# Last stage of a two-block image kernel: one narrow projection for two pairs of images, and stacked rows filled by transfers

## What is computed

```python
r = jnp.einsum('bhwc,cd->bhwd', x, Wr) + br                  # 64 channels to 16
r = jax.nn.relu((r - mean) * jax.lax.rsqrt(var + BN_EPS) * gamma + beta)
w = jnp.einsum('bhwd,dk->bhwk', r, Ws) + bs                  # 16 to 9 taps x 16 groups
xi = jnp.einsum('bhwc,cf->bhwf', x, Wi) + bi                 # 64 to 64
patches = ...                                                # the 9 shifts of padded xi
out = jnp.sum(w * patches, axis=-1)                          # per group of 4 channels
```

## Time and profile before

| what | value |
|---|---|
| median of 3 runs | 675.14 us (674.09 to 675.57) |
| profiled execution, its own time | 673.33 us |
| its span, first to last instruction | 671.5 us |
| mean granted clock of TensorE | 0.985 |
| last stage: first tap of pair 0 to the end | 453.9 to 671.5 us |
| one pair in it, from pair 2 on | 12.74 us |

### The profile page before, as it was taken

How to read it: one execution, slowest core, us unless ns; L and a number is a source line. 1 busy time by engine, 2 the same in 40 slices (tenths; PEclk the granted TensorE clock), 3 DMA queues, 4 the chain that set the end, 5 groups by cost and what they waited for, 6 DMA issues and landing times. The chain is left out here.

```text
span 671.5 us, 15413 instructions
## 1 busy us (share of the span) xinstructions
PE 628.5 (94%) x5984; PEld 250.0 (37%) x5984; DVE 522.5 (78%) x816; ACT 326.7 (49%) x451; POOL 181.0 (27%) x193
## 2 busy tenths in 40 slices
PE   6868999889999999999999989798999999999995
PEld 7523333323333333333333323233444444444442
DVE  5699875997766666766688676969898898888885
ACT  3754632311422242133315545743687787788761
POOL 2100330007300810280047000531344234235231
PEclk9979899999999999999999979999999999999998
DMA  8930030042433253125422416000122222132132
GB/s 323 220 66 1 1 84 1 1 95 71 98 93 73 72 139 101 50 71 141 95 67 55 116 31 149 1 9 9 25 57 48 48 64 48 41 70 49 40 72 63
DMA packets 67461, 47.95 MB, mean 71 GB/s; under 512 B 53602, under 2 KB 54596, under 8 KB 67396
## 3 DMA queue, kind: packets, MB, share of 16 engines
q1 hardware_dynamic: 67108, 46.82, 28.3%
q10 hardware_dynamic: 288, 0.21, 0.1%
HBM read 35.15 MB, written 9.76 MB: 67 GB/s over the span
## 5 line engine op out<-in xcount | busy, mean ns | idle before, releaser
L759 PE MATMUL conv<-xpad,comb 64*64 64x512 f32 x2016 | 228.1, 597 | 4.3 <-DVE x L1386 4.2
L1646 DVE TENSOR_TENSOR x<-conv,x 128x512 f32<-128x512 f32 x288 | 177.9, 683 | 24.0 <-PE conv L814 22.7
L759 PEld LDWEIGHTS conv<-xpad,comb 64*64 64x64 f32 x2016 | 75.4, 134 | 136.6 <-issue 121.7
L814 PE MATMUL conv<-rstack,wse 98*128 98x512 f32 x288 | 95.9, 434 | 2.9 <-DVE xin L1432 0.9
L830 PE MATMUL att<-x,cmp 64*32 64x512 f32 x1280 | 79.7, 596 | 0.0
L814 PEld LDWEIGHTS conv<-rstack,wse 98*128 98x128 f32 x288 | 48.1, 188 | 72.3 <-DVE x L1646 65.7
L1318 DVE SCALAR_TENSOR_TENSOR xpad<-att,x 128x1024 f32<-128x1024 f32 x46 | 54.1, 1219 | 25.7 <-PE att L609 25.3
L960 ACT ACTIVATE x<-conv,bias 128x512 f32<-128x512 f32 x40 | 25.2, 682 | 90.5 <-PE conv L759 90.5
L728 PE MATMUL conv<-row_sums,comb 64*64 64x512 f32 x480 | 58.5, 617 | 9.0 <-DVE xin L1432 7.7
L1798 POOL TENSOR_TENSOR x<-x,xin 128x1024 f32<-128x1024 f32 x15 | 35.9, 2393 | 111.5 <-ACT x L1112 111.5
L951 ACT ACTIVATE comb<-experts,small 128x768 f32<-128x768 f32 (+1 forms) x33 | 27.4, 859 | 78.1 <-PE conv L728 31.9
(11 more groups left out here) (212 smaller groups left out, 749.8 us busy)
## 6 DMA issues: line engine op xcount, KB each, us to landing
experts<-forms SPq DMA_DIRECT2D x72, 192.0 KB, 4.0
experts<-forms SPq DMA_DIRECT2D x72, 144.0 KB, 2.8
x<-in_x SPq DMA_DIRECT2D x32, 256.0 KB, 5.6
out<-comb SPq DMA_DIRECT2D x30, 256.0 KB, 3.2
rstack<-rstack SPq DMA_DIRECT2D x16, 128.0 KB, 2.3
experts<-in_We SPq DMA_DIRECT2D x1, 1152.0 KB
forms<-experts SPq DMA_DIRECT2D x2, 576.0 KB, 5.7
out<-comb SPq DMA_DIRECT2D x4, 128.0 KB, 2.2
```

The costliest lines, as they stand in the source:

```text
L759: last = nc.tensor.matmul(conv[own[to], h, HW * rows:HW * rows + HW], comb[own[rows], q % 2, n, tap(t)], xpad[own[rows], 2 * (q % 2) + n, ...
L814: nc.tensor.matmul(conv[:, unit, cols], wse[:, ORDER[i], :], rstk[s][0:RR, cols], start=True, stop=True).then_inc(exp_full, 1)
L1646: v.tensor_tensor(img(prod[i])[:, rows, :], img(conv[:, unit, :])[:, rows, :], xip[s][:, kh + 16 * h:kh + 16 * h + 16, kw:kw + W], ALU.mul ...
```

## The change

The narrow projection is made for two pairs at once. `wr` has the block once, 32 columns wide, and four matmuls write the two halves of pairs k+1 and k+2 to four blocks of 32 partitions of `att[:, 1, 0:512]`. It is made in odd pairs only, behind the two sums and ahead of tap 2; the place behind tap 3 is gone. ScalarE normalises pair k+2 instead of k+1, takes relu and the rounded copy of both pairs as 128x512 (into `r_lo4` and `r_hi4`), and issues two of the transfers. GpSimd subtracts once for two pairs (`split_two`), ahead of the residual of pair k-1. The stacks are filled by transfers of 32 rows x 512 columns (64 KB): six for each pair, four of slot 0's and six of slot 1's on SyncE (`fill`), which waits for the expansions of pair k-2. `misc_*` counts five uses per two pairs. Some buffers move (`prod`, `xn`).

```diff
-        prod = [flat[:, n * S:(n + 1) * S] for n in (0, 1, 2, 3, 4, 5, 13, 14, 15)]
-        xn = [flat[:, (6 + n) * S:(7 + n) * S] for n in range(2)]
-        r64 = flat[0:TWO, 8 * S:9 * S]
+        prod = [flat[:, n * S:(n + 1) * S] for n in (0, 1, 2, 3, 4, 7, 13, 14, 15)]
+        xn = [flat[:, n * S:(n + 1) * S] for n in (6, 5)]
+        r_lo4 = flat[:, 8 * S:8 * S + HW]
+        r_hi4 = flat[:, 8 * S + HW:9 * S]
...
+        def misc_before(k):
+
+            return 5 * (k // 2) + (4 if k % 2 else 2)
...
-            copy_high(0, 0)
-            copy_high(1, 1)
+            def fill(k, s, made):
+
+                eng.wait_ge(rhi_ready, made)
+                if not (isinstance(k, int) and k < 2):
+                    eng.wait_ge(exp_full, 2 * TAPS * (k - 1))
+                for first, part in ((0, r_hi4), (ONE, r_lo4)) if s == 0 else ((0, r_hi4), (2 * ONE, r_hi4), (ONE, r_lo4)):
+                    if first == ONE:
+                        eng.wait_ge(rlo_ready, made)
+                    for h, cols in halves():
+                        rows = slice(2 * ONE * s + ONE * h, 2 * ONE * s + ONE * h + ONE)
+                        eng.dma_start(rstk[s][first:first + ONE, cols].bitcast(F32), part[rows, :]).then_inc(rstk_filled[s], 16)
+
+            for n in range(2):
+                fill(n, n, 1)
             with eng.Fori(0, GP - 1) as i:
                 for n in range(2):
-                    copy_high(2 * i + n + 2, n)
-                    store_pair(2 * i + n, n, 6 * i + 3 * n + 8)
-            store_pair(NP - 2, 0, 3 * NP)
+                    fill(2 * i + n + 2, n, i + 2)
+                    store_pair(2 * i + n, n, 5 * i + 2 * n + 7)
+            store_pair(NP - 2, 0, MISC_USES)
...
-            def project(k, s, m):
+            def project_two(k, m):
                 if not (isinstance(m, int) and m == 0):
                     eng.wait_ge(misc_free, m)
-                eng.wait_ge(xn_ready, k + 1)
-                for h, cols in halves():
-                    last = nc.tensor.matmul(att[own[h], 1, cols], wr[:, :], xn[s][:, cols], start=True, stop=True)
+                eng.wait_ge(xn_ready, k + 2)
+                for s in range(2):
+                    for h, cols in halves():
+                        first = 2 * ONE * s + ONE * h
+                        last = nc.tensor.matmul(att[first:first + ONE, 1, 0:HW], wr[:, :], xn[s][:, cols], start=True, stop=True)
                 last.then_inc(misc_full, 1)
...
-                    elif at == (3, 0, 6):
+                    elif at == (3, 1, 0):
                         eng.wait_ge(att_free[1], sum(u == 1 for u, _ in ATT_USES))
-                        project(0, 0, 0)
-                    elif at == (3, 1, 2):
+                        project_two(0, 0)
+                    elif at == (3, 1, 3):
                         project_xi(0, 0, 1)
...
                 if i == 0:
-                    eng.wait_ge(rstk_ready, k + 1)
-                    eng.wait_ge(rhi_copied[s], 8 * (k - s) + 16)
+                    eng.wait_ge(rstk_filled[s], FILLS // 2 * (k - s) + FILLS)
...
                 if not first:
                     add_up(k - 1, 3)
                     add_up(k - 1, 4)
+                if s and not last:
+                    project_two(k + 1, m)
                 expand(k, s, 2)
                 expand(k, s, 3)
-                if not last:
-                    project(k + 1, 1 - s, m)
                 expand(k, s, 4)
...
-            def empty_r(k, s, m):
+            def empty_two(made, m):
                 eng.wait_ge(misc_full, m + 1)
-                if not (isinstance(k, int) and k == 0):
-                    eng.wait_ge(rstk_ready, k)
+                if not (isinstance(made, int) and made == 0):
+                    for s in range(2):
+                        eng.wait_ge(rstk_filled[s], FILLS * made)
+                nc.scalar.activation(r_lo4, att[:, 1, 0:HW], ACT.Relu, bias=rsc[:, 3:4], scale=rsc[:, 1:2]).then_inc(misc_free, 1)
+                eng.wait_ge(misc_free, m + 1)
+                nc.scalar.activation(r_hi4.bitcast(F32R), r_lo4, ACT.Copy).then_inc(rhi_ready, 1)
+                eng.wait_ge(rhi_ready, made + 1)
                 for h, cols in halves():
-                    done = nc.scalar.activation(r64[:, cols], att[own[h], 1, cols], ACT.Relu, bias=rsc[own[h], 3:4],
-                                                scale=rsc[own[h], 1:2])
-                done.then_inc(misc_free, 1)
-                eng.wait_ge(misc_free, m + 1)
-                nc.scalar.activation(rstk[s][0:TWO, :], r64, ACT.Copy).then_inc(rhi_ready, 1)
+                    eng.dma_start(rstk[0][2 * ONE:3 * ONE, cols].bitcast(F32), r_hi4[ONE * h:ONE * h + ONE, :])\
+                        .then_inc(rstk_filled[0], 16)
...
+                if not (isinstance(k, int) and k >= NP - 2):
+                    normalise2(k + 2, s)
+                if not (isinstance(k, int) and k == 0):
+                    empty_sum(k - 1)
+                if s and not last:
+                    empty_two(made, m)
                 if not last:
-                    normalise2(k + 1, 1 - s)
...
+            def split_two(made):
+                if isinstance(made, int) and made == 1:
                     eng.wait_ge(nmr_ready, 5)
-                eng.wait_ge(rhi_ready, k + 1)
-                v.tensor_tensor(rstk[s][32:64, :], r64[32:64, :], rstk[s][32:64, :].bitcast(F32), ALU.subtract)\
-                    .then_inc(rstk_ready, 1)
-                eng.wait_ge(rstk_ready, k + 1)
+                eng.wait_ge(rhi_ready, made)
+                v.tensor_tensor(r_lo4.bitcast(F32R), r_lo4, r_hi4, ALU.subtract).then_inc(rlo_ready, 1)
...
             with eng.Fori(0, GP - 1) as i:
-                involve(2 * i + 1, 1)
-                involve(2 * i + 2, 0)
-            involve(NP - 1, 1, last=True)
+                split_two(i + 2)
+                finish(2 * i)
+                finish(2 * i + 1)
+            finish(NP - 2)
```

More of the change, by code:

```diff
@@ L39 @@
 RR = 98
-TWO = 64
+ONE = 32
+FILLS = 16 * 6
+MISC_USES = 40
 T = S // 128
@@ L162, in build @@
         wi = sb("wi", [128, 128])
-        wr = sb("wr", [128, TWO])
+        wr = sb("wr", [128, ONE])
         sw = sb("sw", [128, 2, 32])
@@ L295, in build @@
         rhi_ready = sem("rhi_ready")
-        rhi_copied = [sem("rhi_copied0"), sem("rhi_copied1")]
-        rstk_ready = sem("rstk_ready")
+        rlo_ready = sem("rlo_ready")
+        rstk_filled = [sem("rstk_filled0"), sem("rstk_filled1")]
         exp_full = sem("exp_full")
@@ L401, in build @@
         BLOCKS = [(wi[64 * n:64 * n + 64, 64 * n:64 * n + 64], A["Wi"]) for n in range(2)]
-        BLOCKS += [(wr[64 * n:64 * n + 64, 32 * a + CR * n:32 * a + CR * n + CR], A["Wr"])
-                   for n in range(2) for a in range(2)]
+        BLOCKS += [(wr[64 * n:64 * n + 64, CR * n:CR * n + CR], A["Wr"])
+                   for n in range(2)]
         CONSTS_IN = 16 * (len(CONSTS) + len(BLOCKS))
@@ L475, in store_pair @@
                                   pix[n][:, :, 64 * m:64 * m + 64]).then_inc(stored[n], 16)
-            def copy_high(k, s):
-                eng.wait_ge(rhi_ready, k + 1)
-                eng.dma_start(rstk[s][TWO:AR, :].bitcast(F32), rstk[s][0:TWO // 2, :].bitcast(F32)).then_inc(rhi_copied[s], 16)
-            copy_high(0, 0)
-            copy_high(1, 1)
+            def fill(k, s, made):
[10 more added lines that the diff above has]
+                fill(n, n, 1)
             with eng.Fori(0, GP - 1) as i:
                 for n in range(2):
-                    copy_high(2 * i + n + 2, n)
-                    store_pair(2 * i + n, n, 6 * i + 3 * n + 8)
-            store_pair(NP - 2, 0, 3 * NP)
+                    fill(2 * i + n + 2, n, i + 2)
+                    store_pair(2 * i + n, n, 5 * i + 2 * n + 7)
+            store_pair(NP - 2, 0, MISC_USES)
             for h in range(2):
@@ L832, in add_up, with involve @@
                 last.then_inc(sum_done, 1)
-            def involve(k, s, first=False, last=False):
-                m = 2 if first else 3 * k + 2
+            def involve(k, s, m, first=False, last=False):
                 expand(k, s, 0)
@@ L850, in involve @@
                 if not last:
-                    project_xi(k + 1, 1 - s, m + 1)
+                    project_xi(k + 1, 1 - s, m + s)
                 expand(k, s, 6)
@@ L857, in involve @@
                 if not first:
-                    turn_back(k - 1, m if last else m + 2)
+                    turn_back(k - 1, m if last else m + s + 1)
             eng.wait_ge(wse_ready, 1)
             eng.wait_ge(late_setup, LATE_STEPS)
-            involve(0, 0, first=True)
-            eng.wait_ge(misc_free, 4)
+            involve(0, 0, 2, first=True)
+            eng.wait_ge(misc_free, 3)
             eng.wait_ge(late_mv_ready, GP + QP)
@@ L869, in _ @@
             for k in range(1, NP):
-                involve(k, k % 2, last=(k == NP - 1))
+                involve(k, k % 2, misc_before(k), last=(k == NP - 1))
```

(71 more changed lines are left out.)

## The result

The changed kernel takes 685.57 us (median; 684.8 to 686.3) where the kernel before takes 675.12: slower by 10.45, ratio 1.0157 (95% interval 1.0139 to 1.0174). Forecast were 681.2, slower, with a range of 679.0 to 688.0. The profiled execution takes 685.44, its span 683.6, which is 12.1 longer than before.

A forecast was written before the change was run, and what follows sets the result against it. VectorE's products bound taps 2 to 5, TensorE merely kept busy. 6 x 1.00 + 0.34 - 0.26 = +6.1 on 673.33 gives 679.4; with 1.81 to the median, 681.2. Own range 679.4 to 683.2, stated range 679.0 to 688.0.

The forecast's parts named there:

- C: Rival: the fills on SyncE's queue come late; each us past 1.8 of cover costs seven, 1 late is 688; chance 0.05.
- D: Rival: the new projection's four column blocks don't run side by side; P = 2.0, sum 13.1, 688.2; chance 0.03.
- Even pairs, 0: Pairs 2 to 14 lose a projection that filled a wait for VectorE in taps 2 to 5: 0, bounds 0 and +0.07 each.
- the sum of 3.08: From tap 2's start to the last half of tap 5, set by VectorE's products: 0.54 + 3 x 0.60 + 0.68 + 0.06.
- Odd pairs, P = 1.00: New projection ahead of tap 2, uncovered, lengthens each odd pair by its price P: 1.00, bounds 0.87 and 1.08.
- Pair 1, +0.34: VectorE is behind by the group norm and reaches tap 2 late, so pair 1 is only 0.34 longer.
- The start, -0.26: Projection three taps later; VectorE, which stood 0.26, meets the last convolution's end: -0.26, between 0 and -0.39.
- ScalarE, GpSimd, SyncE, 0: Normalising, copies, subtraction, residual and transfers of the new order are all covered in time: counted 0.
- The cover on the fills: SyncE's transfers land at 11.9 (13.1), tap 0 of the next pair is at 13.75: covered by 1.8 (0.6).
- The sum, +6.1: Whole kernel: 6 x 1.00 + 0.34 - 0.26 = +6.1 us, low 5.0, high 7.4.
- A: Rival: TensorE is the bound, fourteen projections of 1.01 go and seven of 1.00 come: -7.1 us, 668.0; chance 0.10.
- B: Rival: VectorE is the bound and its backlog in odd pairs swallows the projection: no change, 675; chance 0.06.

The follow-up runs named there:

- the old place: Changed kernel with the projection for two pairs put back behind tap 3 of odd pairs: 674.60 us, ratio 1.0009 against the kernel before.
- two fillers: The old place plus two idle projections behind tap 3 of even pairs and pair 0: span 676.5 against 673.2 (one execution).
- fillers in all pairs: Changed kernel with four idle matmuls of the projection's shape behind tap 3 of every pair but the last: 680.30 us, ratio 1.0093 against the kernel before.
- the removal alone: Kernel before, with the narrow projection of odd pairs (made in even pairs and pair 0) cut to 16 of 512 columns a half: 674.81 us, ratio 1.0011.
- the place alone: Kernel before, with the narrow projection made in odd pairs moved from behind tap 3 to ahead of tap 2: 681.32 us, ratio 1.0105.
- fillers in even pairs: Changed kernel with four idle matmuls behind tap 3 of every even pair and pair 0: 683.59 us, ratio 1.0131 against the kernel before.
- the sums apart: The old place, the wide projection of even pairs and pair 0 moved behind tap 3, and tap 2 between the sums of rounds 3 and 4: 671.65 us, ratio 0.9970.

## Why the prediction was right, and what it left out

The 685.57 lies within the stated range, but above the 683.2 at which the forecast's own range ended. It lies within only because the range was drawn on to 688.0 to hold the rivals C and D. Neither happened, so that part is luck. The mechanism of odd and even pairs is not.

**Even pairs, 0.** Right. From pair 2 on, two kernels without the projection there and two with an idle one in its place all have 12.74 to 12.78, but for pair 14 of the changed kernel, where the clock fell. One reading in the working is off: the 0.81 that the weight loads stood ahead of tap 4 was not for VectorE. The product that tap 4 needs first began at 562.76 and took 0.68, so it was done by 563.44, while TensorE was at the projection until 564.36. Only the 0.41 ahead of the last half of tap 5 is VectorE's, and the sum of 3.08 rests on that one. Nor do pairs take 12.74 from pair 1 on, but from pair 2 on; pair 1 took 13.89.

**Odd pairs, P = 1.00.** Right: where the clock did not fall, odd pairs from pair 3 on are 0.98 to 1.04 longer, in the changed kernel and with the old projection in the new place alone. The choice of 1.00 over 0.87 was right: the new projection took 1.00 behind the sums. It is a rule of the Trainium skill (TensorEngine Tiling (Array Packing), Key Properties), a drain at a change of tiling mode, that had favoured it, and this trace agrees: 1.00 between other shapes, 0.87 in a row of its own shape.

**Pair 1, +0.34.** 14.22 for 13.89: +0.33.

**The start, -0.26.** Tap 0 of pair 0 came at 454.26 instead of 453.91, but the last convolution had begun 0.83 later (436.31, 435.48) for reasons ahead of the change. Against that beginning it is -0.48, more than the 0.26 that was taken and than the bound of 0.39. The premise that VectorE meets the end of that convolution fell away: it stood 3.23 there instead of 0.26 (last section).

**ScalarE, GpSimd, SyncE, 0.** Right for the time, as the kernel with the old place shows. The cover on the fills was thinner than worked out in some pairs: in pair 9 they landed some 1.0 us ahead of tap 0, not 1.8. The first two issues on SyncE took 2.65 there, where 2 x 0.59 was put down. In the changed kernel they took 1.3 in pairs 1, 3, 7 and 11 and 2.2 to 2.7 in pairs 5, 9 and 13, beside ScalarE's two each time; why is open. In the kernel with two fillers slow issues on ScalarE did cost time.

**The sum, +6.1.** The terms for the pairs came true: +6.0 in odd pairs 3 to 13, +0.33 in pair 1. The step that failed is one that I took without a term: that the granted clock stays 1.00 in the last stage as it was in the earlier trace rows. Falls cost 1.6 each in pairs 11 and 14 and 1.67 in pair 0 (16.65 for 14.98 from tap 0 to tap 0), 4.9 of the 12.1 in the profiled execution; the rest are small differences, +0.35 up to tap 0, +0.2 over six even pairs and +0.3 at the end. Over runs the kernel with fillers in all pairs lies 6.3 above the kernel before (ratio 1.0093), close to the forecast's 6.1, and the changed kernel lies 4.3 above that one, which is what the forecast lacked.

**The rivals.** A, TensorE's work taken out as time gained, is refuted by the old place and by the removal alone, which gain nothing. B needs a backlog that pair 9 does not have (VectorE stands 1.51). C did not happen; D did not (1.00).

**What is shown of the falls, and what is open.** The traces of all ten kernels hold seven falls in pairs 1 to 14, each at the end of bare taps 2 to 5. In 98 pairs with something between taps 3 and 4 there was none. (The 16 columns left in the removal are counted as bare.) In these traces, then, a fall in pairs 1 to 14 needs the bare taps, in which the weight loads wait 0.4 to 0.5 for VectorE ahead of single expansions. The idle matmuls in every pair bear it out: with taps 2 to 5 of all these pairs filled, no fall was left in the profiled execution, and the runs lay within 1.2 us. The bare taps are not enough: 35 pairs had them without a fall. Six of the seven falls were in the 21 odd pairs with a projection ahead of the bare taps (one in the changed kernel, two with the place alone, three with fillers in even pairs). The seventh was in pair 14 of the changed kernel, which has none ahead; it was the only one in 21 such even pairs. That the projection ahead makes falls more frequent is likely by these counts, but no run tests it alone. Why one such pair falls and the next does not stays open.

So does pair 0. It took 16.4 to 16.7 in the changed kernel and the experiments with the old place, with the removal alone and with fillers in even pairs, and 15.0 in the others. The clock fell there in some of these others as well (0.77 with the place alone, with fillers in every pair and with the sums apart) and cost nothing. With fillers in even pairs and in all pairs TensorE does the same work in pair 0 (only the columns of its idle results differ), and one took 16.49, the other 15.00. So the loss of 1.67 there can't be put down to the change.

## What to carry over

A busy engine need not be the bound: cut the stage where the other engine hands back buffers, and see whether work taken out lets the next instruction start sooner. Here one place hid up to about 1.2 us of TensorE's work; taking work from it gave nothing, moving work out of it to a place where VectorE had run dry cost its whole length, and filling it with needed work gave 0.6 a pair. When a change leaves TensorE waiting between single matmuls, read the granted clock pair by pair and give it a term of its own.

## What the runs showed of the hardware

The granted clock of TensorE can fall to its lower level with the engine busy for most of the stretch: pairs at 0.89 hold matmuls over 97% of their time (14.98 of 15.36), and each fall there cost 1.6 us. A pair at full clock shows the same share (13.36 of 13.75 in pair 9), so the busy time doesn't give a fall away. Adding idle matmuls in every pair made the changed kernel 4.3 us faster by the two ratios.

VectorE's addition of 128x2048 (the residual of the last convolutions, both inputs in SBUF) took 4.09 us while GpSimd's subtraction ran from 446.05 to 448.40 in the kernel before, and 2.28 in the changed kernel, where GpSimd was idle until 447.80. With the place alone, which keeps the old order of GpSimd, it took 4.08. The rows are VectorE and GpSimd before, then VectorE after:

```profile
446.47 4.09 DVE L1456 TENSOR_TENSOR xin<-xin,x 128x2048 f32<-128x2048 f32 x1
...
446.05 2.35 POOL L1791 TENSOR_TENSOR rstack<-x,rstack 32x1024 fp32r<-32x1024 f32 x1 [5.41 <-ACT rstack L1104]
```

```profile
445.66 2.28 DVE L1476 TENSOR_TENSOR xin<-xin,x 128x2048 f32<-128x2048 f32 x1
```

The 1.81 between them is about the time that GpSimd's instruction still had to run when VectorE's began (446.47 to 448.40). The Trainium skill (SBUF — State Buffer, Who interferes with whom) says that of a VectorE instruction with two SBUF inputs and a GpSimd instruction that reads SBUF the second waits for the first; these rows agree. These 1.81 are one of two reasons why VectorE no longer met the end of the last convolution. The other is that the first half of it no longer holds the narrow projection: VectorE had its result 8.03 after the convolution began (436.31 to 444.34), 9.66 before (435.48 to 445.14). That is 1.63 more room. By these numbers either alone would have kept VectorE off the path, so the start came 0.48 instead of 0.26 earlier.
